# Windowed attention in units of one image and one channel half, remade in units of two images

## The reference

```
q = (x @ Wq + bq).reshape(B, S, H, hd).transpose(0, 2, 1, 3)
...
scores = jnp.einsum('bhqd,bhkd->bhqk', q, k) * scale
...
allowed = (j <= i) & (i - j < WINDOW)
scores = jnp.where(allowed, scores, NEG_INF)
attn = jax.nn.softmax(scores, axis=-1)
out = jnp.einsum('bhqk,bhkd->bhqd', attn, v)
```

## Time and profile before

| | before |
|---|---|
| median of 3 runs | 1057.77 us (1054.72 to 1058.64) |
| the profiled execution | 1058.27 us, of which the span is 1056.5 us |
| attention stage | 51.6 to 224.4 us of the span |
| TensorE, VectorE, ScalarE, GpSimd busy over the span | 90%, 56%, 39%, 49% |

### The profile page before, as it was taken

The page is one execution under the profiler, slowest core; times in us unless marked ns, Lnnn a source line. Parts: engine busy times, 40 slices in busy tenths (PEclk is TensorE's granted clock), DMA queues, the critical chain, the costliest instruction groups (busy, mean ns, idle before and its releaser), DMA issues. The chain is left out here.

```text
span 1056.5 us, 29782 instructions
## 1 busy us (share of the span) xinstructions
PE 950.1 (90%) x10440; PEld 746.9 (71%) x10440; DVE 589.3 (56%) x1463; ACT 412.9 (39%) x1102; POOL 522.1 (49%) x714
## 2 busy tenths in 40 slices
PE   8899999988747999999999999889979947999996
PEld 6667777777634888888888876445546635888895
DVE  1878888865994777433333325678877552111111
ACT  2266776634253344444444422223323222433331
POOL 0056655610604777776777627777773002433332
PEclk9999999999979999999999999989889987999998
DMA  7010000002004988877788723334482046486750
GB/s 257 1 46 2 0 0 0 2 11 75 1 1 165 307 275 254 277 243 224 242 264 255 228 88 100 101 115 120 121 288 82 22 182 228 143 271 215 266 155 26
DMA packets 79821, 149.30 MB, mean 141 GB/s; under 512 B 18892, under 2 KB 53327, under 8 KB 75760
## 3 DMA queue, kind: packets, MB, share of 16 engines
q1 hardware_dynamic: 34768, 77.15, 21.5%
q0 software_dynamic: 17712, 47.88, 15.8%
q10 hardware_dynamic: 27248, 23.09, 6.5%
HBM read 200.22 MB, written 31.73 MB: 220 GB/s over the span
## 5 line engine op out<-in xcount | busy, mean ns | idle before, releaser
L1332 POOL DMA_INDIRECT x_x<-m_x_rows,x_idx x170 | 166.1, 977 | 74.3 <-issue 35.8
L1358 PE MATMUL x_pup<-x_xt,x_w 128*128 128x128 f32 (+1 forms) x2176 | 182.9, 250 | 0.0
L1358 PEld LDWEIGHTS x_pup<-x_xt,x_w 128*128 128x128 f32 (+1 forms) x2176 | 166.9, 165 | 5.9 <-issue 5.7
L1624 POOL DMA_INDIRECT rl_y<-m_y_rows,rl_idx x136 | 134.8, 991 | 43.6 <-issue 37.8
L1439 DVE TENSOR_TENSOR x_hid<-x_gate,x_pup 128x128 f32<-128x128 f32 x170 | 48.9, 288 | 148.2 <-ACT x_gate L1411 142.4
L1372 PE MATMUL x_pdown<-x_w,x_hid 128*128 128x256 f32 (+1 forms) x408 | 104.2, 389 | 0.2 <-DVE x_y L1446 0.2
L1407 ACT ACTIVATE x_xt<-x_pturn 128x256 f32<-128x256 f32 x170 | 65.3, 384 | 89.1 <-PE x_pturn L1343 86.3
L442 POOL TENSOR_TENSOR wa_probs<-wa_probs,wa_peak 68x544 f32<-68x544 f32 x64 | 70.0, 1094 | 57.5 <-DVE wa_peak L593 54.7
L2437 DVE TENSOR_TENSOR x_y<-x_pdown,x_b 128x256 f32<-128x256 f32 x21 | 8.9, 425 | 150.7 <-PE x_pdown L2391 150.7
L2423 ACT ACTIVATE x_hid<-x_pup,x_b 128x128 f32<-128x128 f32 (+1 forms) x200 | 52.8, 357 | 93.7 <-PE x_pup L2374 93.5
L1411 ACT ACTIVATE x_gate<-x_pup 128x128 f32<-128x128 f32 x170 | 47.2, 278 | 92.4 <-PE x_pup L1358 92.4
(11 more groups left out here) (344 smaller groups left out, 1914.8 us busy)
## 6 DMA issues: line engine op xcount, KB each, us to landing
x_w<-in_experts SPq DMA_DIRECT2D x204, 384.0 KB
late_w<-in_w SPq DMA_DIRECT2D x28, 1024.0 KB, 13.3
m_y_rows<-x_y ACTq DMA_DIRECT2D x170, 128.0 KB
xT<-in_w SPq DMA_DIRECT2D x12, 1024.0 KB, 6.1
xn<-in_w SPq DMA_DIRECT2D x10, 1024.0 KB, 10.3
h<-in_w SPq DMA_DIRECT2D x10, 1024.0 KB, 14.0
m_x_rows<-xn SPq DMA_DIRECT2D x34, 128.0 KB, 1.8
x_x<-m_x_rows,x_idx POOLq DMA_INDIRECT x170
```

The costliest lines, as they stand in the source:

```text
L1332: nc.gpsimd.indirect_dma_start(x[:, s, :], None, x_rows, bass.IndirectOffsetOnAxis(ap=idx[:, s:s + 1], axis=0))\
L1358: mm = nc.tensor.matmul(pup[rows:rows + wide, bank, m * P + side * wide:m * P + (side + 1) * wide], w[:, lane, first:first + wide], xt[:, ...
L1624: nc.gpsimd.indirect_dma_start(y[:, t % YR, kk, :], None, y_rows, bass.IndirectOffsetOnAxis(ap=idx[:, n:n + 1], axis=0))\
```

## The change

A unit is now two images and one chunk, so there are 32 units, in steps that are all written out. Only queries and keys 0 to 63 are in it: image 0 takes the partitions 0 to 63 and image 1 those from 64, and every elementwise operation works on 128 partitions x 512 instead of 68 x 544. The sums come from VectorE, which adds up the exponentials (`add_up`) and inverts them for 8 heads at once (`invert`); GpSimd multiplies the probabilities by them before they are turned (`normalise`). So the products with ones, the 128 x 68 inversion and the 128 x 68 multiplication are gone, and one turn takes two heads of two images at once (4 turns of 128 x 128).

The queries 64 to 67 of two images and 16 heads make 128 rows, which are handled once in two steps, with 68 keys each: `last_spread` (GpSimd), 4 score products, `last_mask`, `last_peak`, `last_exp`, `last_invert`, `last_normalise` (GpSimd, three operations), then `last_turn`, two products with a constant `row_sel` that select and turn the rows at once, `last_move`, `last_weigh` (24 products of 8 or 4 columns) and `last_place`. The values of the tokens 64 to 67 get a job of their own, `vt`, for four images. The value jobs are now two, for two images each. Where a step has two jobs, the second stands behind the turn.

```diff
-        "mask": np.where((k <= q) & (q - k < WINDOW), 0.0, NEG),
+        "mask": np.where((k2 <= q2) & (q2 - k2 < WINDOW), 0.0, NEG),
+        "last_mask": np.where((k <= HALF + row_query) & (HALF + row_query - k < WINDOW), 0.0, NEG),
...
+        plast = st.enter_context(nc.psum_tensor("wa_last", [P, 512], fp32))
+        pl_score = pscore[:, 0, P:P + S]
+        pl_main, pl_tail, pl_out = plast[:, 0:HALF], plast[0:HALF, HALF:P], plast[:, P:P + 16]
...
+        def jobs_of(step):
+            blk, n = step // ABLK, step % ABLK
+            if step >= STEPS:
+                return []
+            jobs = [[(blk, "v0"), (blk + 1, "q0")], [(blk, "v1"), (blk + 1, "q1")],
+                    [(blk, "vt"), (blk + 1, "k0")], [(blk + 1, "k1")]][n]
+            return [job for job in jobs if job[0] < NBLK]
...
+                def spread(unit):
+                    c = unit % DC
+                    pool.wait_ge(jobs_moved, done_by(unit, f"k{c}"))
+                    if unit >= 2:
+                        pool.wait_ge(scored, unit - 1)
+                    keys = pair_cols(unit, slice(0, HALF))(kT[:, unit // ABLK % 2, c, :])
+                    for i in range(2):
+                        ins = nc.gpsimd.tensor_tensor(
+                            kheads[:, unit % 2, i, :, :], keys[:, i, :].unsqueeze(1).broadcast_to([P, PER, HALF]),
+                            const("head_of").unsqueeze(2).broadcast_to([P, PER, HALF]), ALU.mult)
+                    ins.then_inc(keys_spread, 1)
...
+                def last_normalise(pair):
+                    pool.wait_ge(l_inverted, pair + 1)
+                    if pair:
+                        pool.wait_ge(l_turned, pair)
+                    nc.gpsimd.tensor_tensor(lrows[:, :], const("row_tail"), linv[:, 0:1].broadcast_to([P, 18]), ALU.mult)                        .then_inc(l_rows, 1)
+                    pool.wait_ge(l_rows, pair + 1)
+                    if not pair:
+                        pool.wait_ge(vals_set, 3)
+                    nc.gpsimd.tensor_tensor(ltail[:, :, 0:ABLK * LAST].rearrange("p o (n q) -> p o n q", q=LAST),
+                                            lprob[:, pair % 2, HALF:S].unsqueeze(1).unsqueeze(1).broadcast_to([P, 2, ABLK, LAST]),
+                                            lrows[:, pair % 2 * 8:pair % 2 * 8 + 8].rearrange("p (o n) -> p o n", n=ABLK)
+                                            .unsqueeze(3).broadcast_to([P, 2, ABLK, LAST]), ALU.mult)
+                    nc.gpsimd.tensor_tensor(lmain[:, :, :], lprob[:, pair % 2, 0:HALF].unsqueeze(1).broadcast_to([P, 2, HALF]),
+                                            lrows[:, 16:18].unsqueeze(2).broadcast_to([P, 2, HALF]),
+                                            ALU.mult).then_inc(l_ready, 1)
+                for step in range(STEPS + 1):
+                    even = step % 2 == 0
+                    if step < STEPS:
+                        shift(step)
+                    if step >= 1:
+                        normalise(step - 1)
+                    if even and 2 <= step <= STEPS:
+                        last_normalise(step // 2 - 1)
+                    if not even and (step + 1) // 2 < NPAIR:
+                        last_spread((step + 1) // 2)
+                    if step + 2 < STEPS:
+                        spread(step + 2)
...
+                    for n in range(2):
+                        first = blk * CB + (2 * int(kind[1]) + n) * S
+                        for kc in range(DC):
+                            for odd in range(2):
+                                mm = nc.tensor.matmul(pjob[odd * HALF:(odd + 1) * HALF, n * P:(n + 1) * P],
+                                                      xT[:, kc, first:first + HALF], wv[:, kc, odd * P:(odd + 1) * P],
+                                                      start=(kc == 0), stop=(kc == DC - 1))
...
+                    pe.wait_ge(normalised, unit + 1)
+                    if unit:
+                        pe.wait_ge(turn_moved, unit)
+                    for two in range(HC // 2):
+                        mm = nc.tensor.transpose(pturn[:, two * P:(two + 1) * P],
+                                                 probs[:, unit % 4, 2 * two:2 * two + 2, :].rearrange("p h n -> p (h n)"), ident)
+                    mm.then_inc(turned, 1)
+                def weigh(unit):
+                    c, slot, pair = unit % DC, unit // ABLK % 2, unit // DC % (ABLK // 2)
+                    pe.wait_ge(turn_moved, unit + 1)
+                    pe.wait_ge(jobs_moved, done_by(unit, f"v{pair}"))
+                    if unit:
+                        pe.wait_ge(placed, unit)
+                    for i in range(2):
+                        for two in range(HC // 2):
+                            mm = nc.tensor.matmul(pout[two * STRIP:(two + 1) * STRIP, i * HALF:(i + 1) * HALF],
+                                                  vals[:, slot, 2 * pair + i, c * (HC // 2) + two, :],
+                                                  probsT[:, unit % 2, two, i, :], start=True, stop=True)
+                    mm.then_inc(weighted, 1)
...
+                    nc.tensor.matmul(pl_main, lmain[:, :, :].rearrange("p o n -> p (o n)"), const("row_sel"), start=True, stop=True)
+                    nc.tensor.matmul(pl_tail, ltail[:, :, :].rearrange("p o n -> p (o n)"), const("row_sel"),
+                                     start=True, stop=True).then_inc(l_turned, 1)
...
+                    for c in range(DC):
+                        for two in range(HC // 2):
+                            at = c * LROWS + two * 8
+                            nc.tensor.matmul(pl_out[two * STRIP:(two + 1) * STRIP, c * 8:(c + 1) * 8],
+                                             vtail[:, slot, c * (HC // 2) + two, :], ltailT[:, at:at + 2 * LAST],
+                                             start=True, stop=False)
+                        for i in range(2):
+                            for two in range(HC // 2):
+                                at = c * LROWS + two * 8 + i * LAST
+                                mm = nc.tensor.matmul(
+                                    pl_out[two * STRIP:(two + 1) * STRIP, c * 8 + i * LAST:c * 8 + (i + 1) * LAST],
+                                    vals[:, slot, first + i, c * (HC // 2) + two, :], lmainT[:, at:at + LAST],
+                                    start=False, stop=(i == 1))
...
+                for step in range(STEPS + 3):
+                    odd = step % 2
+                    jobs = jobs_of(step)
+                    if step < STEPS:
+                        score(step)
+                    if 0 <= step - 3 < STEPS:
+                        weigh(step - 3)
+                    for job in jobs[:1]:
+                        do_job(*job)
+                    if step >= STEPS:
+                        keep_running(3)
+                    if 0 <= step - 2 < STEPS:
+                        turn(step - 2)
+                    for job in jobs[1:]:
+                        do_job(*job)
+                    if odd and 3 <= step < STEPS + 3:
+                        last_turn((step - 3) // 2)
+                    if not odd and 4 <= step < STEPS + 4:
+                        last_weigh((step - 4) // 2)
+                keep_running(3)
...
+                def last_exp(pair):
+                    act.wait_ge(l_peaked, pair + 1)
+                    nc.scalar.activation(lneg[:, :], lpeak[:, :], ACT.Copy, scale=-scale).then_inc(l_negated, 1)
+                    act.wait_ge(l_negated, pair + 1)
+                    if pair >= 2:
+                        act.wait_ge(l_inverted, pair - 1)
+                    nc.scalar.activation(lprob[:, pair % 2, :], lprob[:, pair % 2, :], ACT.Exp, bias=lneg[:, 0:1], scale=scale,
+                                         accum_out=lsum[:, pair % 2:pair % 2 + 1]).then_inc(l_exped, 1)
...
+                for step in range(STEPS + 4):
+                    even = step % 2 == 0
+                    jobs = jobs_of(step)
+                    if even and step >= 4:
+                        last_move((step - 4) // 2)
+                    if not even and step >= 5:
+                        last_place((step - 5) // 2)
+                    if 0 <= step - 3 < STEPS:
+                        place(step - 3)
+                    if 1 <= step <= STEPS:
+                        exp(step - 1)
+                    if not even and step <= STEPS:
+                        last_exp((step - 1) // 2)
+                    for job in jobs[:1]:
+                        move_job(*job)
+                    if 0 <= step - 2 < STEPS:
+                        move_turned(step - 2)
+                    for job in jobs[1:]:
+                        move_job(*job)
```

More of the change, by code:

```diff
@@ new lines, in window_attention @@
+        FIRST = [(0, "k0"), (0, "q0"), (0, "k1"), (0, "q1")]
+        def jobs_of(step):
[5 more added lines that the diff above has]
+            return [job for job in jobs if job[0] < NBLK]
```

(53 more changed lines are left out.)

428 lines of the change are left out of this document (219 added, 209 removed).

## The result

| | before | changed |
|---|---|---|
| median | 1057.77 us | 1047.10 us (1043.28 to 1047.95, 3 runs) |
| the profiled execution | 1058.27, span 1056.5 | 1047.95, span 1046.2 |
| attention stage | 172.8 us | 159.5 us (51.81 to 211.29) |

The ratio is 0.9888, with a 95% interval of 0.9863 to 0.9914: faster by 1.1%, 10.7 us. The forecast was 37 us, with a range of 1004 to 1043; the result lies outside. In the trace the stage is 13.3 us shorter, not 37.6, and the span 10.3. Of the other 3 us, about 1.6 are 32 products of the last stage that took 5.44 us instead of 3.81 because the granted clock fell there in this execution. It is the scatter of executions, and I count only the stage.

What follows compares the result with a forecast made beforehand. TensorE's list was taken to bound the attention stage; 13.6 us plus 2.3 of waits made 15.9 a block, and with start and end the stage ended 37.6 us earlier: 1021 us, range 1004 to 1043.

Steps and rivals of the forecast that it cites:

- the start: Attention stage's first steps: scores 0 at 55.3 us, then the chain's speed rules, not TensorE's; step 4 at 69.5.
- six blocks: Middle of the attention stage: six blocks of four steps, 16.0 us each, running to 165.5 us.
- the drain: Step 31's chain to the stage's end, from 176.4 us: 10.4 us, with 0.7 for filler products; end at 186.8.
- the clock: Granted clock in the attention stage: 0.93 throughout would cost some 5 us, left to the range; no chance given.
- GpSimd holds: Attention steps: GpSimd delivers in time; scores need `spread` of two steps before, turns need `normalise`, done at 4.3, wanted at 5.8.
- the engines meet less well: Rival, attention blocks: ScalarE, GpSimd and TensorE in fixed orders lose more than 2.3 a block; 16 us more, 1037; chance 0.13.
- TensorE's list of 13.6 us: Summed price of TensorE's operations for four images, one block: 13.6 us, where the block before took 20.6.
- The waits for `pjob`: TensorE's q or k jobs wait for ScalarE: 0.4, 1.0, 0.5 in a block's first three steps; 2.3 with lateness handed on.
- The halves of the array: Scores and v jobs: half-width work overlaps; rival that it does not: 28 us more, 1049, chance 0.06.
- the slower one: Rival in `last_weigh`: each of 48 records costs 108 ns instead of 19; 68 us more, 1089; chance 0.06.
- The other engines': Busy times for four images, one block: GpSimd 14.6 us, ScalarE 13.7, VectorE 9.7.
- The floor of GpSimd: GpSimd's 14.6 us a block, 3.65 a step, as the attention stage's floor; it sets the last block's three steps.

## Why the prediction was wrong

The stage ends 24.5 us later than forecast (211.29 for 186.8). By the starts of the scores: the start 3.0 (step 4 at 72.53 for 69.5), six blocks 13.8, the last block's three steps 1.4, the drain 6.2. By causes: 12.2 are the wait for `lq`, 5.4 the clock, and the other 6.9 are terms that were too small in the blocks (2.9), the start (1.9) and the drain (3.1), less 1.0 in the last block, which took 9.9 without the wait where 10.9 were forecast.

- **The step that failed** is "GpSimd holds: TensorE's scores of a step need `spread` of two steps before". True of `spread`; `last_spread`, which TensorE needs within the same `score`, is made one step ahead and in a queue behind 2.1 us of other work. I had its duration (0.58) in GpSimd's sum and never asked when it was due. It is shown: moving it alone gives back 12.2 us of waits, half of the miss (14 us by the medians, where the clock helped). My rival "the engines meet less well" had a size (16 us) near the blocks' 13.8, but named ScalarE's many small operations; that the size was near is luck.
- **The clock** had no term in the sum. I wrote that 0.93 over the whole stage would cost some 5 us and that a fall would be a sign of being wrong, and left it to the range. It fell to 0.90 in the start, 0.77 in step 12 and 0.79 in the drain, and cost some 1.1, 1.2 and 3.1 us there: 5.4. The first and the last are the differences to a like stretch at 1.00; the second is 7.48 less the 6.32 of the other blocks.
- **TensorE's list of 13.6 us** was 14.5, in the earlier trace rows's manner from start to start. Jobs are 1.02 to 1.11 instead of 0.90 to 0.92, 0.8 a block, and `last_turn` is 0.52 for 0.33, 0.4 a block; each step's turns are 0.43. `last_weigh` was 0.83 each for 0.92; scores 0.40 as said; weighing 0.23 to 0.37 for 0.31. Six blocks at 0.9 more are 5.4 us, of which some 2.5 came back by the shorter waits (next point) and by the 16.0 that I had rounded up to.
- **The waits for `pjob`**, 2.3 with what ScalarE hands on, were 2.0 (0.5, 0.85 and 0.65, counted as the time from the start of the turns to the second job, less 0.43; 0.4, 1.0 and 0.5 were forecast, and 0.4 handed on). The mechanism was right and so was its size. With the failed step mended, the block is 16.48 for the 16.0 forecast.
- **The halves of the array** overlap in both new shapes: 16 records of 128 columns in 0.40 us (scores) and 1.02 (v). Rival excluded. So is the slower one, and TensorE's list as the bound of a block is shown by the doubled `last_weigh`. By the Trainium skill's page "TensorE: Matmul & The Clock Gate", section "Wait — 56ns, not 53.3ns?", 48 matmuls would take an estimated 1.2 us at the least. The trace has 0.83, 17 ns a record, and doesn't agree if a record is counted as a matmul. Counted by the kernel's 24 products, of two records each, it is 35 ns, and there is no disagreement; no run here tells which count the page means.
- **The start** was 3.0 us late. 0.3 of them were there at step 0's scores (55.64 for 55.3), and 1.1 are the clock. The other 1.5 are my chain, which was too short at several hand-overs; no run singles one out. The order of q and v is worth 0.2 (16.77 to 16.53 at the same clock).
- **The drain** of 10.4 us was 16.6 and is 13.5 at the full clock. I counted 0.7 for fillers and there are four groups of 1.4, two of them ahead of work that was ready and one ahead of the next stage. The removal of three gave 1.3 of 4.2 us, at a lower clock. The clock's part is seen from executions with all four groups: 13.5 at 1.00, 14.9 at 0.89, 16.6 at 0.79. So 3.1 of the 6.2 are the clock, and 3.1 would be missing without it.
- **The other engines'** busy times were too high: 13.6 for GpSimd's 14.6, 11.9 for ScalarE's 13.7, 9.1 for VectorE's 9.7. The floor of GpSimd was no bound, in the blocks by the run with `normalise` on VectorE, and in the last block, where my 3.65 a step became 3.3, 2.8 and 3.8 once the wait was gone.

## What to carry to other kernels

For each operand that the engine at the bound waits for, write down in which step it is made, behind what in its maker's queue, and in which step it is wanted: two products of the same kind can have a step of slack and none. A signal given only behind a second group (scores, then the last queries' scores) makes the first group's readers wait for the second's operand. When an engine that was 99% busy falls to 85% and nobody else fills up, look at its list of waits before any busy time, and move the late operation forward in its queue before making it faster.

## What the runs showed of the hardware

- A matmul record with 32 weight columns in four column groups starts every 17.3 ns with 4 or 8 data columns, in this kernel, at a granted clock of 1.00.
- The granted clock fell to half (0.50 from 197.2 to 204.0 us of the changed kernel's trace) in some executions and not in others of nearly the same code. In the drain the mean was 0.59 to 0.89 in seven traces and 1.00 in four. In the start it was 0.90 in seven traces without filler products and 1.00 in two, and 1.00 in both traces with them; in the drain it fell with fillers too.
- What that costs depends on who waits. In the start 0.90 instead of 1.00 cost 1.15 us of 15.4; in the drain 0.79 instead of 1.00 cost 3.1 of 13.5.
- VectorE's product over 128 x 512 in SBUF and GpSimd's two head-mask products took longer side by side than apart: 0.81 us for 0.69, and 1.21 for 0.76. Beside VectorE's `mask`, which reads PSUM, GpSimd's two took 0.76.
